# Three TensorE products with no reader, placed in the stage that transposes the cosine output

## The chip, the cores and the metric

The kernel runs on 1 core of one Trainium2 chip. The metric is the device time of one execution in microseconds; lower is better. TensorE (PE in the rows, its weight loads PEld), VectorE (DVE), ScalarE (ACT), GpSimd (POOL) and SyncE (SP) each follow a queue of their own and meet at semaphores.

## The reference

Two transformer layers on x of 32 batches x 256 rows x 128 channels, all in float32. In layer 0 two attentions and a mixture of experts read the same normalised rows:

```python
xn = layernorm(x)
Q, K = l2norm(heads(Wq)), l2norm(heads(Wk)); V = heads(Wv)        # 16 heads of 8
cos = clip(Q K^T, -0.999, 0.999)
W = maximum(1 - arccos(cos) / pi, EPS) ** 16; W = W / (sum(W) + EPS)
cosine_out = (W V) @ Wo.T + bo
softmax_out = softmax(q k^T / sqrt(8)) v
moe_out = top-2 of 8 experts of xn, weighted by the gate
x1 = x + cosine_out + softmax_out + moe_out
```

Layer 1 is a causal attention with one head of 128 and a gated feed-forward layer (352 wide) whose operands are quantised to FP4 in blocks of 16; both read layernorm(x1) and are added to x1.

## The kernel before, in words

The kernel walks the 32 batches one by one. All weights stay in SBUF: among them the identity `ident` (128x128, float32) and the experts' weights `we` (128 x 8 x 128). The work on a batch is cut into stages, and the table `ORDER` writes out by hand, for each engine, in which order the stages stand in one turn of the loop and for which batch: an entry (stage, part, lag) of turn t works on batch t + lag. Each engine follows its list strictly, so what stands behind a waiting stage waits too.

Around the change TensorE's list reads: projection 1 of the next batch, `e 1`, `finc`, `o1`, `ocT`, `e 2`, `e 3`, `wo`. The stages are:

- `e` (lines 1089 to 1098) makes softmax scores for two heads in one of two slots of `psS`. ScalarE's stage `e` (line 670) takes their exponential into `prob`; its list reads `proj 1`, `e 1`, `ln 2`, `gexp`, `e 2`, `e 3`, `guess`, `ln1`.
- `finc` (lines 1105 to 1115) transposes the sums of the cosine attention into a bank of PSUM. VectorE then adds, inverts and multiplies (lines 903, 905 and 907); the last of the three, line 907, writes the finished cosine output `oc` and brings the semaphore `s_finc` to 3 for this batch.
- `o1` (lines 1167 to 1175) is the value product of layer 1's attention for the batch before; VectorE reads it at lines 962 and 966.
- `ocT` (lines 1116 to 1123) transposes `oc`. VectorE copies the result to `ocT` (line 993).
- `wo` (lines 1124 to 1131) multiplies with Wo; VectorE adds the result to the residual as `x1` (line 921), from which layer 1 starts. All of layer 1's normalisation follows from `x1`.

VectorE's list reads `proj 1`, `gmax`, `quanth 8`, `finc`, `o1`, `ocT`, `norm`, `wo`, `ln1`. At line 797 it adds the bias to a projection that TensorE makes at line 1037.

The stages other than the scores share two banks of PSUM (`psM`), 512 float32 columns each. Uses are numbered through TensorE's list (`MISC`), and even numbers take one bank, odd ones the other. In one turn, the last use of projection 1 has number 12, `finc` 13, `o1` 14, `ocT` 15 and `wo` 16. Before a stage writes its bank it waits until the last user of that bank has been read; `bank_read` walks back two numbers and returns the semaphore and value of that reader:

```python
("down", 0, 0): (s_y, 1), ("finc", 0, 0): (s_finc, 3), ("finf", 0, 0): (s_finf, 2),
...
return psM[n % 2], n % 2
```

`due(s, b)` is the value that semaphore s has once batch b is done; `s_finc` counts 3 in a batch. `ocT` uses 256 columns of its bank (T = 256); columns 256 to 511 are not used by it.

In the rows, a float32 product shows as two matmuls, each with a weight load, and a transpose as one. Line 1145 (`p1`) is the one product in the loop whose stationary operand is 128x128 and whose moving operand has 256 columns in float32; line 1150 is the next in TensorE's queue behind it. Activations all stand at line 578, and their tiles tell them apart.

Of the kernel before, what the change touches and what calls it, by code (L numbers as in the profile page):

```python
# [111 lines left out]
def build(nc, x, Wq, Wk, Wv, Wo, bo, W_qkv, b_qkv, W_gate, b_gate, W_experts, b_experts,  # L112
          w_qkv1, w_out1, w_gate1, w_up1, w_down1, y):
    B, T, _ = x.shape
# [7 lines left out]
    with ExitStack() as ctx:  # L122
        def sb(name, shape, dt=F32):
            return ctx.enter_context(nc.sbuf_tensor(name, shape, dt))
# [11 lines left out]
        def due(s, b, n=None):  # L136

            value = b * per[s.name] + (per[s.name] if n is None else n)
            return max(value, 0) if isinstance(value, int) else value
# [15 lines left out]
        ident = sb("ident", [P, P])  # L155
# [9 lines left out]
        we = sb("we", [P, E, D])  # L165
# [164 lines left out]
        def head_window(v, k, j, head):  # L330

            e = head % 2
            return v[:, k, j, head // 2, :, :].rearrange("p t c -> p (t c)")[:, e * HALF_GROUP:e * HALF_GROUP + FULL_GROUP]

        def head_at(g, hh):

            return 8 * (g // 2) + 2 * hh + g % 2
# [17 lines left out]
        def misc_bank(stage, arg, use):  # L355
            n = MISC.index((stage, arg, use))
            return psM[n % 2], n % 2
# [17 lines left out]
        def bank_read(stage, arg, use, t, uses=MISC):  # L375

            n = uses.index((stage, arg, use))
            ring = [k for k in range(len(uses)) if k % 2 == n % 2]
            at = ring.index(n)
            for back in range(1, 4 * len(ring)):  # L380
                k, turns = ring[(at - back) % len(ring)], -((at - back) // len(ring))
                entry = t - turns + LAG[uses[k][:2]]
                if not isinstance(entry, int) or 0 <= entry < B:
                    s, event = READ[uses[k]]
                    return s, due(s, entry, event)
                if t - turns < -1:
                    break
            return s_wcp, SETUP_USES
# [610 lines left out]
        def _(pe):  # L999
            mm, transpose = nc.tensor.matmul, nc.tensor.transpose  # L1000
            pe.wait_ge(s_const, due(s_const, 0))
            pe.wait_ge(s_w, due(s_w, 0, 16 * WEIGHT_DMAS))
            for n in range(SETUP_USES):
                src, dst = (TRANSPOSES + BIAS_ROWS + PRODUCTS)[n][0], (TRANSPOSES + BIAS_ROWS + PRODUCTS)[n][-1]
                bank = psM[n % 2][0:dst.shape[0], 0:dst.shape[1]]
# [13 lines left out]
            def rows(hh):  # L1019
                return slice(FULL_GROUP * hh, FULL_GROUP * (hh + 1))  # L1020

            def run(stage, arg, b, p, t):
                if stage == "xnT":
                    bank, k = misc_bank(stage, 0, 0)
# [6 lines left out]
                if stage == "proj":  # L1031
                    pe.wait_ge(s_xnT, due(s_xnT, b))
                    for use, w, n in ((0, w0T[:, :, :].rearrange("p k n -> p (k n)"), 3 * D), (1, wf[:, :], 3 * D + E)):
                        bank, k = misc_bank(stage, arg, use)
# [3 lines left out]
                if stage == "experts":  # L1038

                    for j in range(NT):  # L1040
                        bank, k = misc_bank(stage, arg, j)
# [5 lines left out]
                if stage == "stackT":  # L1047
                    kind = KINDS[arg]
                    bank, k = misc_bank(stage, arg, 0)
# [12 lines left out]
                if stage == "c":  # L1062

                    pe.wait_ge(s_stkT, due(s_stkT, b))
                    for kt in range(NT):
                        for a in range(2):
                            hh = 2 * (arg % 2) + a
                            ins = mm(psS[:, slot, a, kt, :], stkT[rows(hh), 1, g, kt * P:(kt + 1) * P], stkT[rows(hh), 0, g, :],  # L1068
                                     start=True, stop=True)
                    ins.then_inc(s_c, 1)  # L1070
                if stage == "m":

                    pe.wait_ge(s_stkT, due(s_stkT, b, 2))
                    for qt_ in range(NT):
                        for a in range(2):
                            hh = 2 * (arg % 2) + a
                            ins = mm(psS[:, slot, a, qt_, :], stkT[rows(hh), 2, g, qt_ * P:(qt_ + 1) * P], stkT[rows(hh), 3, g, :],  # L1077
                                     start=True, stop=True)
                    ins.then_inc(s_m, 1)
                if stage == "maxT":  # L1080
                    bank, k = misc_bank(stage, 0, 0)
# [7 lines left out]
                if stage == "e":  # L1089

                    pe.wait_ge(s_mT, due(s_mT, b))
                    for kt in range(NT):
                        for a in range(2):
                            hh = 2 * (arg % 2) + a
                            mm(psS[:, slot, a, kt, :], stkT[rows(hh), 3, g, kt * P:(kt + 1) * P], stkT[rows(hh), 2, g, :],  # L1095
                               start=True, stop=False)
                            ins = mm(psS[:, slot, a, kt, :], pickb[rows(hh), g, :], mT[rows(hh), :], start=False, stop=True)  # L1097
                    ins.then_inc(s_e, 1)
                if stage == "pvf":
                    pv(arg, prob[:, 2 * (arg % 2):2 * (arg % 2) + 2, :].rearrange("p u c -> p (u c)"), vf, s_prob, 2 * arg + 2, s_pvf,  # L1100
                       b, p)
                if stage == "pvw":
                    pe.wait_ge(s_qkc, due(s_qkc, b))
                    pv(arg, curve[:, p, 2 * arg * UC:2 * (arg + 1) * UC], vc, s_pow, arg + 1, s_pvc, b, p)
                if stage in ("finc", "finf"):
                    src, ready, done = (oCs, s_oC, s_fincp) if stage == "finc" else (oFs, s_oF, s_finfp)
                    pe.wait_ge(ready, due(ready, b))
                    bank, k = misc_bank(stage, arg, 0)
# [7 lines left out]
                if stage == "ocT":  # L1116
                    bank, k = misc_bank(stage, 0, 0)
                    last, value = bank_read(stage, 0, 0, t)
                    pe.wait_ge(last, value)
                    pe.wait_ge(s_finc, due(s_finc, b))  # L1120
                    for j in range(NT):
                        ins = transpose(bank[:, j * P:(j + 1) * P], oc[:, j, :], ident[:, :])
                    ins.then_inc(s_ocTp, 1)
                if stage == "wo":
                    bank, k = misc_bank(stage, 0, 0)
# [6 lines left out]
                if stage == "xn1T":  # L1132
                    bank, k = misc_bank(stage, 0, 0)
# [6 lines left out]
                if stage == "p1":  # L1140
                    bank, k = misc_bank(stage, 0, 0)
# [4 lines left out]
                    bank, k = misc_bank(stage, 0, 1)  # L1146
# [5 lines left out]
                if stage == "s1":  # L1152
                    bank, k = misc_bank(stage, 0, 0)
# [5 lines left out]
                if stage == "p1T":  # L1159
                    bank, k = misc_bank(stage, 0, 0)  # L1160
# [6 lines left out]
                if stage == "o1":  # L1167
                    bank, k = misc_bank(stage, 0, 0)
# [7 lines left out]
                if stage == "xqT":  # L1176
                    bank, k = misc_bank(stage, 0, 0)
# [6 lines left out]
                if stage == "gu":  # L1184
                    pe.wait_ge(s_xqT, due(s_xqT, b))
                    for m in range(2):
                        bank, k = misc_bank(stage, arg, m)
# [4 lines left out]
                if stage == "hT":  # L1192
                    pe.wait_ge(s_qh, due(s_qh, b))
                    bank, k = misc_bank(stage, arg, 0)
# [5 lines left out]
                if stage == "down":  # L1200
                    bank, k = misc_bank(stage, 0, 0)
# [3 lines left out]
                    for j in range(NT):  # L1205
                        for c in range(NCH):
                            ins = mm(bank[:, j * D:(j + 1) * D], hqT[0:CH[c], j, c, :], wdT[0:CH[c], c, :],  # L1207
                                     start=(c == 0), stop=(c == NCH - 1))
                    ins.then_inc(s_dnp, 1)

            def pv(g, weights, v, ready, event, done, b, p):

                half = g // 2
                kind, copied = (0, s_oC) if v is vc else (1, s_oF)
                pe.wait_ge(ready, due(ready, b, event))
                if g == 0:
                    pe.wait_ge(copied, due(copied, b - 1))
                w = weights.rearrange("p (h k q) -> p h k q", h=4, k=NT)
                for kt in range(NT):
                    for hh in range(4):  # L1220
                        ins = mm(psV[rows(hh), kind, half, :], head_window(v, p, kt, head_at(g, hh)), w[:, hh, kt, :],  # L1221
                                 start=(g % 2 == 0 and kt == 0), stop=(g % 2 == 1 and kt == NT - 1),
                                 tile_position=(0, FULL_GROUP * hh))
                ins.then_inc(done, 1)

            steps(pe, ORDER["tensor"], run)


# [19 lines left out]
```

## Time and profile before

| what | value |
|---|---|
| median of 3 runs | 1970.91 us (1962.58 to 1976.08) |
| the profiled execution's own time | 1969.34 us |
| its span, first to last instruction | 1967.5 us |
| mean granted clock of TensorE | 0.85 of full speed |
| VectorE busy | 1766.3 us (90%) |
| ScalarE busy | 1765.2 us (90%) |
| TensorE busy (matmuls) | 1486.0 us (76%) |

A busy share is an average over the whole span. Which engine holds the others up at one place is read from the waits, the chain that ended last and the timeline there. A granted clock of 1.00 is 2.4 GHz and one of 0.50 is 1.2 GHz; values between are mixtures of the two in one stretch.

### The profile page before, as it was taken

The numbers are of one execution on the slowest core, as the hardware profiler recorded it, in microseconds if no ns is written. First come the engines' busy times: TensorE is split into PE (matmuls) and PEld (weight loads), VectorE is DVE, ScalarE is ACT, GpSimd is POOL, SyncE is SP. The second block draws the span as 40 slices with busy tenths as digits, with TensorE's granted clock in tenths as the row PEclk, the third lists the DMA queues.
The fourth block names the chain that finished last, engine by engine and source line by source line (L and its number), as shares of the span: only waits on it lengthen the run. The fifth ranks groups of instructions, "written<-read, shape, count | busy, mean of one in ns | idle before, by whom it ended". The sixth has DMA issues, their size and how long they took to land.

```text
span 1967.5 us, 38505 instructions
## 1 busy us (share of the span) xinstructions
PE 1486.0 (76%) x12022; PEld 752.9 (38%) x12022; DVE 1766.3 (90%) x4009; ACT 1765.2 (90%) x1856; POOL 1182.2 (60%) x540
## 2 busy tenths in 40 slices
PE   2667787777777877777787787878777787777766
PEld 1223434333443433344343344343334434333433
DVE  5779999999999999999999999999999999999864
ACT  1299999999999999999999999899999999999893
POOL 1566666666666566566656666665667666665640
PEclk9578889889889888888978888897888889888776
DMA  1000000000000000000000000000000000000000
GB/s 42 3 4 1 6 1 6 5 6 6 6 3 3 6 5 6 6 6 0 6 6 5 6 5 6 0 6 6 5 6 5 6 0 6 6 5 6 4 3 6
DMA packets 21058, 11.19 MB, mean 6 GB/s; under 512 B 1431, under 2 KB 20953, under 8 KB 20956
## 3 DMA queue, kind: packets, MB, share of 16 engines
q1 hardware_dynamic: 20956, 10.20, 1.8%
q14 instruction: 83, 0.68, 0.1%
q8 instruction: 19, 0.31, 0.1%
HBM read 6.00 MB, written 4.19 MB: 5 GB/s over the span
## 4 chain that ended last, share of the span: by engine, by line
DVE 34%; ACT 24%; issue 22%; PE 16%; DVEq 1%; POOL 1%; SPq 0%; ACTq 0%; DMA 0%; POOLq 0%
ACT curve L578 13%; DVE nmax L880 6%; DVE curve L870 5%; ACT root L578 4%; PE psM L1037 3%; PE psM L1045 3%; DVE curve L874 3%; DVE acc L854 2%; PE psM L1190 1%; DVE stkT L866 1%; DVE xn L776 1%; ACT prob L578 1%; ACT L609 1%; PE psS L1095 1%; DVE h L454 1%
## 5 line engine op out<-in xcount | busy, mean ns | idle before, releaser
L530 POOL TENSOR_TENSOR root<-curve 128x2048 f32<-128x2048 f32 x128 | 478.7, 3740 | 453.1 <-DVE curve L874 453.1
L578 ACT ACTIVATE curve<-curve 128x2048 f32<-128x2048 f32 x384 | 718.8, 1907 | 5.5 <-POOL curve L533 2.2
L578 ACT ACTIVATE root<-root 128x2048 f32<-128x2048 f32 x256 | 484.6, 1906 | 0.0
L533 POOL TENSOR_TENSOR curve<-curve,root 128x2048 f32<-128x2048 f32 x64 | 354.5, 5562 | 64.4 <-ACT root L578 64.4
L578 ACT ACTIVATE prob<-psS 128x1024 f32<-128x1024 f32 x256 | 256.7, 1029 | 66.1 <-PE psS L1097 63.9
L874 DVE TENSOR_SCALAR curve<-psS 128x1024 f32<-128x1024 f32 x256 | 308.4, 1216 | 2.7 <-PE psS L1068 2.7
L880 DVE TENSOR_REDUCE nmax<-psS 128x4 f32<-128x1024 f32 x256 | 303.0, 1215 | 1.0 <-PE psS L1077 1.0
L566 POOL TENSOR_TENSOR stk<-qk,stk 128x512 f16<-128x512 f32 x128 | 147.8, 1164 | 76.9 <-ACT stk L578 76.6
L1045 PE MATMUL psM<-we,xnT 128*128 128x512 f32 x256 | 168.8, 747 | 0.0
L870 DVE TENSOR_TENSOR curve<-curve,root 128x2048 f32<-128x2048 f32 x64 | 162.0, 2531 | 6.1 <-ACT root L578 6.1
L1221 PE MATMUL psV<-curve,vc 128*32 128x256 f32 x2048 | 140.8, 406 | 29.8 <-ACT curve L578 25.9
L1077 PE MATMUL psS<-stkT 32*128 32x256 f16 x1024 | 105.7, 300 | 71.5 <-DVE curve L874 36.8
L1190 PE MATMUL psM<-wguT,xqT 128*128 128x352 f32 x256 | 131.7, 654 | 36.4 <-ACT hqT L578 32.8
L1221 PE MATMUL psV<-prob,vf 128*32 128x256 f32 x2048 | 153.7, 423 | 0.6 <-ACT prob L578 0.6
L854 DVE SCALAR_TENSOR_TENSOR acc<-psM,comb,acc 128x128 f32<-128x128 f32 x512 | 137.7, 340 | 11.7 <-PE psM L1045 11.7
L1207 PE MATMUL psM<-wdT,hqT 128*128 128x128 f32 (+1 forms) x384 | 91.8, 428 | 61.8 <-DVE h L972 61.1
L1068 PE MATMUL psS<-stkT 32*128 32x256 f16 x1024 | 107.6, 314 | 21.1 <-DVE curve L874 10.4
L1207 PEld LDWEIGHTS psM<-wdT,hqT 128*128 128x128 f32 (+1 forms) x384 | 82.5, 323 | 76.5 <-DVE h L972 75.4
L1056 PE MATMUL psM<-ident,stk 128*128 128x128 f16 x1024 | 81.2, 224 | 34.3 <-ACT xn1T L578 26.6
L1095 PE MATMUL psS<-stkT 32*128 32x256 f16 x1024 | 102.3, 299 | 4.5 <-ACT prob L578 3.3
L1221 PEld LDWEIGHTS psV<-curve,vc 128*32 128x32 f32 x2048 | 61.1, 114 | 107.2 <-issue 80.2
L1097 PE MATMUL psS<-mT,pickb 32*128 32x256 bf16 x1024 | 101.4, 297 | 0.0
(194 smaller groups left out, 2800.2 us busy)
## 6 DMA issues: line engine op xcount, KB each, us to landing
xt<-in_L_attn_x SPq DMA_DIRECT2D x32, 128.0 KB, 2.1
out<-yo SPq DMA_DIRECT2D x32, 128.0 KB, 1.8
we<-in_L_ffn_W_experts SPq DMA_DIRECT2D x1, 512.0 KB
curve<-in_L_attn_w_qkv SPq DMA_DIRECT2D x1, 192.0 KB
curve<-in_L_ffn_w_down SPq DMA_DIRECT2D x1, 176.0 KB
curve<-in_L_ffn_w_gate SPq DMA_DIRECT2D x2, 64.0 KB
curve<-in_L_ffn_w_up SPq DMA_DIRECT2D x2, 64.0 KB
curve<-in_L_ffn_W_qkv SPq DMA_DIRECT2D x1, 128.0 KB
```

The costliest lines, as they stand in the source:

```text
L530: nc.gpsimd.tensor_tensor(root[:, two], curve[:, p, two], curve[:, p, two], ALU.mult).then_inc(s_sq, 1)
L533: nc.gpsimd.tensor_tensor(curve[:, p, two], curve[:, p, two], root[:, two], ALU.mult).then_inc(s_half[0], 1)
L566: nc.gpsimd.tensor_tensor(lo, src, hi, ALU.subtract).then_inc(s_stk, 1)
L578: return nc.scalar.activation(out, in_, func, **kw)
L854: nc.vector.scalar_tensor_tensor(acc[:, p, j, :], bank[:, (e % 4) * D:(e % 4 + 1) * D], comb[:, p, j, e:e + 1], acc[:, p, j, :], ALU.mult, ...
L870: nc.vector.tensor_tensor(curve[:, p, two], curve[:, p, two], root[:, two], ALU.mult).then_inc(s_half[1], 1)
L874: nc.vector.tensor_scalar(curve[:, p, arg * UC:(arg + 1) * UC], psS[:, slot_of(stage, arg), :, :, :].rearrange("p a k q -> p (a k q)"), CO ...
L880: nc.vector.tensor_reduce(nmax[:, :, 2 * arg:2 * arg + 2].rearrange("p j a -> p a j"), psS[:, slot_of(stage, arg), :, :, :], AX.X, ALU.max ...
L1045: mm(bank[:, :], xnT[:, j * P:(j + 1) * P], we[:, 4 * arg:4 * arg + 4, :].rearrange("p e f -> p (e f)"), start=False, stop=True).then_inc( ...
L1190: ins = mm(bank[:, 0:I], xqT[:, arg * P:(arg + 1) * P], wguT[:, m, :], start=True, stop=True)
L1207: ins = mm(bank[:, j * D:(j + 1) * D], hqT[0:CH[c], j, c, :], wdT[0:CH[c], c, :], start=(c == 0), stop=(c == NCH - 1))
L1221: ins = mm(psV[rows(hh), kind, half, :], head_window(v, p, kt, head_at(g, hh)), w[:, hh, kt, :], start=(g % 2 == 0 and kt == 0), stop=(g % ...
```

## The change

In the stage `ocT`, between the wait for the bank and the wait for the cosine output, TensorE runs three products of `ident` with the first two experts' weights (256 columns). They are written to columns 256 to 511 of the stage's bank, each over the one before, and nothing reads them.

```diff
                     bank, k = misc_bank(stage, 0, 0)
                     last, value = bank_read(stage, 0, 0, t)
                     pe.wait_ge(last, value)
+                    keep_clock(bank[:, T:2 * T], 3)
                     pe.wait_ge(s_finc, due(s_finc, b))
                     for j in range(NT):
                         ins = transpose(bank[:, j * P:(j + 1) * P], oc[:, j, :], ident[:, :])
                     ins.then_inc(s_ocTp, 1)
...
+            def keep_clock(spare_psum, count):
+
+                for k in range(count):
+                    mm(spare_psum, ident[:, :], we[:, 0:2, :].rearrange("p e f -> p (e f)"), start=True, stop=True)
```

## Rows read from the trace of the kernel before

**Rows 1.** The page: busy time of each engine, share of the span, instructions.

```profile
PE 1486.0 (76%) x12022; PEld 752.9 (38%) x12022; DVE 1766.3 (90%) x4009; ACT 1765.2 (90%) x1856; POOL 1182.2 (60%) x540
```

**Rows 2.** Waits, whole span: who waited for whom, us in total, times, longest.

```profile
ACT prob L578 <- PE psS L1097: 63.9, 77, 1.8
...
DVE qk L797 <- PE psM L1037: 61.0, 40, 4.3
...
PE psM L1122 <- DVE oc L907: 51.3, 30, 2.1
```

**Rows 3.** Chain that ended last, 1070 to 1082 us: start, us, what.

```profile
1075.46 0.44 DVE oc L907
...
1076.03 0.41 PE psM L1122 x2
1076.44 0.24 PE psS L1095 x4
```

**Rows 4.** Timeline, 323 to 328 us: start, length, instruction, [idle before <-releaser].

```profile
323.53 0.39 PE L1175 MATMUL psM<-v,p1T 128*128 128x129 f32 x2
...
324.97 0.42 DVE L907 TENSOR_TENSOR oc<-psM,rsC 128x256 f32<-128x256 f32 x1
...
325.55 0.41 PE L1122 MATMUL psM<-ident,oc 128*128 128x128 f32 x2 [1.63 <-DVE oc L907]
...
326.04 0.42 DVE L993 COPY ocT<-psM 128x256 f32<-128x256 f32 x1
...
326.55 1.94 ACT L578 ACTIVATE prob<-psS 128x1024 f32<-128x1024 f32 x2 [0.92 <-PE psS L1097]
...
327.41 0.42 DVE L921 TENSOR_TENSOR x<-psM,acc 128x256 f32<-128x256 f32 x1
```

**Rows 5.** Timeline, 381 to 386 us: the same stage one batch later.

```profile
381.97 0.42 DVE L907 TENSOR_TENSOR oc<-psM,rsC 128x256 f32<-128x256 f32 x1
...
382.54 0.66 PE L1122 MATMUL psM<-ident,oc 128*128 128x128 f32 x2 [1.88 <-DVE oc L907]
...
384.21 1.94 ACT L578 ACTIVATE prob<-psS 128x1024 f32<-128x1024 f32 x2 [1.84 <-PE psS L1097]
...
385.43 0.41 DVE L921 TENSOR_TENSOR x<-psM,acc 128x256 f32<-128x256 f32 x1
```

**Rows 6.** Stretches between ends of line 907: length; PE, PEld, DVE, ACT, POOL busy; clock.

```profile
325.39:382.39 57.00, 44.22 (x375) 22.62 (x375) 53.59 (x125) 54.86 (x59) 36.98 (x17) 0.88 0.02 5
382.39:440.46 58.07, 45.61 (x375) 23.30 (x375) 54.85 (x125) 54.83 (x57) 36.76 (x17) 0.85 0.02 5
728.01:785.08 57.07, 44.27 (x375) 22.62 (x375) 53.73 (x125) 55.15 (x59) 36.86 (x17) 0.88 0.02 5
785.08:843.11 58.03, 45.60 (x375) 23.24 (x375) 54.64 (x124) 54.91 (x58) 36.77 (x17) 0.85 0.02 5
```

**Rows 7.** The same columns, for 0.9 and for 2.0 us from line 907's end.

```profile
382.39:383.29 0.90, 0.75 (x6) 0.45 (x10) 0.74 (x5) 0.00 (x0) 0.90 (x1) 0.51 0.00 0
...
1933.50:1934.40 0.90, 0.81 (x3) 0.29 (x2) 0.69 (x4) 0.00 (x0) 0.00 (x0) 0.50 0.00 0
...
152.35:154.35 2.00, 1.81 (x22) 1.32 (x22) 1.37 (x4) 1.70 (x3) 2.00 (x3) 0.84 0.00 0
...
1933.50:1935.50 2.00, 1.33 (x5) 0.84 (x5) 1.12 (x5) 0.00 (x0) 0.00 (x0) 0.50 0.00 0
```

**Rows 8.** Line 1145 in all (ns min/median/max), and two timelines.

```profile
L1145 PE MATMUL psM<-xn1T,wqk x64: 379/468/763, 164.1 to 1941.2; 128*128 128x256 f32 x64
...
1086.63 0.70 PE L1145 MATMUL psM<-xn1T,wqk 128*128 128x256 f32 x2
1087.17 0.61 PE L1150 MATMUL psM<-wvo,xn1T 128*128 128x128 f32 x4
...
1940.61 1.19 PE L1145 MATMUL psM<-xn1T,wqk 128*128 128x256 f32 x2 [0.56 <-ACT xn1T L578]
...
1941.59 1.06 PE L1150 MATMUL psM<-wvo,xn1T 128*128 128x128 f32 x4
```

## The prediction, made before the change was run

> **What bounds the kernel now.** I read the page first. VectorE and ScalarE are both busy for 90% of the span, TensorE for 76% [rows 1]. Shares don't say who waits at the place of the change, so the view of the waits came next. It has both sides of the stage `ocT` near its top: TensorE waits 51.3 us in all for the cosine output (line 907), and ScalarE waits 63.9 us for scores (line 1097) [rows 2]. The chain that ended last shows that these are one story: from line 907 it goes to the two transposes at line 1122, and on to the scores at line 1095 that stand behind them in TensorE's queue [rows 3].
>
> The timeline of one batch has the times [rows 4]. The last product of `o1` ends at 323.92 us (323.53 + 0.39), line 907 ends at 325.39, and the transposes start at 325.55: TensorE idled 1.63 us. The exponential of `e 2` starts at 326.55, and ScalarE had stood idle for 0.92 us, because `e 2` is queued behind the transposes. VectorE's copy at line 993 starts at 326.04 with no idle time ahead of it, and `x1` (line 921) follows at 327.41. So VectorE has next to no slack here, and ScalarE has less than none.
>
> Is a delay at this place passed on to the next batch? The trace holds a test. One batch later the granted clock is 0.51 in the stretch right behind line 907 [rows 7], so the same work is late [rows 5]: line 907 ends at 382.39, and the exponential starts 1.82 us behind it instead of 1.16, `x1` 3.04 us behind it instead of 2.02. The first batch lasted 57.00 us from line 907 to line 907, the one that was slowed 58.07; another such pair has 57.07 and 58.03 [rows 6]. A delay of 0.7 us for ScalarE and 1.0 us for `x1` made the batch 1.0 us longer. Nothing later took it back: ScalarE's idle time outside this one wait is 57.00 - 54.86 - 0.92 = 1.22 us in the first batch and 58.07 - 54.83 - 1.84 = 1.40 us in the second [rows 4 to 6].
>
> **What the change does.** It means to fill TensorE's 1.63 us of idling. What decides is when the wait ahead of the products ends. It waits for the reader of the bank's last user. The uses alternate between two banks, and `finc` has number 13, `o1` 14, `ocT` 15. So the last user of `ocT`'s bank is `finc` of the same batch, and its reader is done when `s_finc` stands at 3, which is the end of line 907. The wait behind the products asks for the same value of the same semaphore. **Both waits end together, and the three products run after the wait and not in it.** The idling stays whole, and the products stand between the cosine output and the transposes.
>
> A rule of the Trainium skill says why no earlier wait would do ("PSUM — Partial Sum Buffer", section "PSUM bank collisions raise a hardware error"): engines have to be kept apart by bank and quadrant, not by address, so the unused columns of a bank that VectorE is reading are not free to write. No row of before shows what happens otherwise.
>
> **The price of the products.** Each batch gets three products, which are six matmuls and six weight loads. The nearest row has the same shape, line 1145. At full clock its two matmuls take 0.54 us until line 1150 starts (1086.63 to 1087.17). The second one ends at 1087.33 and lasts 0.38, so it started 0.32 us behind the first, and line 1150 came 0.22 us after that [rows 8]. In a run of six, I take it that only the first has the longer step, since the later weight loads lie under the matmul ahead: 0.32 + 5 x 0.22 = 1.42 us. The other end is 3 x 0.54 = 1.62 us, every pair like that at line 1145. I take 1.42. At the low clock the pair takes 0.98 us (1940.61 to 1941.59) [rows 8], so three cost at most 2.94, and by twice 1.42 they cost 2.84.
>
> Nothing is removed or moved, and there is no DMA, no new wait and no new semaphore. `ident` and `we` lie in SBUF. The second wait is met already when TensorE comes to it; I cost it at nothing, since TensorE's queue is then full of the products.
>
> **Who pays.** The transposes, `e 2`, `e 3` and `wo` start 1.42 us later. ScalarE's wait for `e 2` grows from 0.92 to about 2.3 us in the batch shown, and VectorE waits about 1.4 us at line 993 where it waited for nothing. Both are late together. VectorE has another wait in the batch, at line 797, of 1.5 us on average (61.0 / 40) [rows 2]. That one is for a projection whose operand ScalarE copies, and ScalarE is just as late, so it doesn't take the delay back. With a delay passed on in full, 32 x 1.42 = **45 us**.
>
> **The clock.** In the 0.9 us behind line 907 the granted clock is below 1.00 in 11 of the 32 batches, and in the 2.0 us behind it in 20; the first and the last of each are shown [rows 7]. Two things follow, with opposite signs.
> - Against: in the 11 batches the products cost 2.84 us and not 1.42, at most 11 x 1.42 = 16 us. Most of that is not new: while the products use up the time at the low clock, the transposes and scores behind them get less of it, and it cost them 1.0 us in such a batch before [rows 6]. In the other 9 the fall now meets the transposes and scores, at up to 1.0 us each, 9 us. I take 20 us for the sum at its worst.
> - For: the products are work where there was none so early, and could keep the clock from falling. At 1.0 us for each of the 20 batches [rows 6, 7] that is 20 us at most. It can't reach a fall that comes at the end of line 907 itself [rows 5, 7], because no product has run by then.
>
> I take zero for the sum of the two, and keep -20 and +20 for the range. The forecast is 1969.3 + 45 = **2014 us** against the profiled execution's 1969.34, which lies 1.6 us below the median of the runs.
>
> **Rivals.**
> 1. *The clock is held.* For it: the clock falls behind an idle stretch, at a place where the products add work. The cost remains, 45 - 20 = +25 us, **1994 us**. The skill has a rule on this side ("TensorE: Matmul & The Clock Gate", section "What's actually happening"): the low level is the default, and activity lifts it. That the clock is low behind this wait in 20 batches [rows 7] agrees with it; by it alone the time would be this rival's.
> 2. *The delay is absorbed: not slower.* VectorE's 1.5 us at line 797 [rows 2] and ScalarE's other 1.2 to 1.4 us of idling in a batch [rows 4 to 6] are of the size of the delay. They would hide it if each engine took its own share back there. It decides if less than 0.44 of the delay is passed on (19.7 of 45 us). The time would lie between 1969 and 1989 us, **1979 us** in the middle. Against it stand the two pairs of batches, which passed on all of it [rows 6].
> 3. *The clock gets worse.* If the low level comes at the end of line 907 in every batch, the products cost 32 x 2.84 = 91 us, less 1.0 us for each of the 20 batches that paid for it before: +71 us, **2040 us**.
> 4. *It does what it says.* If the first wait ended earlier, the products would lie in the 1.63 us of idling and cost next to nothing, and up to 20 us of low clock would go: **1955 us**, with 14 us in place of 20. The numbering of the banks speaks against it.
>
> **How the numbers follow.** Forecast 0.68, rival 1 0.13, rival 2 0.11, rival 3 0.05, rival 4 0.03. 1% of the median is 19.7 us, about what a measurement of this kernel can tell from no change, so the border is at 1990.6 us. The forecast, rival 3 and most of rival 1 lie above it: slower 0.86. Rival 2 lies within 1%: 0.11. Faster by over 1% is rival 4: 0.03. The range goes from 1988 us (rival 1 with 6 us of the delay absorbed) to 2036 us (the forecast with the full +20 of the clock).
>
> **What would show it.** In the profile after, the matmuls of the new line start about 0.15 us behind the end of line 907, not behind the last product of `o1`, and the idling ahead of them is still put down to line 907. From line 907's end to the transposes it is some 1.6 us and not 0.16. ScalarE's wait for line 1097 grows by about 45 us in all, VectorE waits at line 993, and a batch lasts about 59 us. I am wrong if the products start while line 907 still runs, if a batch lasts no longer although the transposes are late (absorbed), or if the granted clock behind line 907 changes in so many batches that it outweighs 45 us.

## The result, and the profile after

The change made the kernel slower: 2002.77 us in the median of four executions (1995.63 to 2019.77) against 1971.35 us before. The ratio is 1.0177, with an interval of 1.01 to 1.0254. The forecast was 2014 us, its range 1988 to 2036. The direction and the size were right. The composition was not: in the profiled execution most of the time was lost in four of the 32 batches, by something that the prediction didn't know of, while the delay that it counted cost on balance a quarter of what it said. When the same kernel was measured again (experiment 9) its ratio was 1.0075; there two of five executions, 2013.87 and 2050.23 us, lie over 1.5% above the fastest and are left out as disturbed, though no trace says whether they were that or had more of those long batches.

The profiled execution after is the slowest of the four, 2019.77 us, 50.43 us above the one before (1969.34). All readings of after are from it. Its page, as [rows 1], with the span:

```profile
span 2018.0 us, 38857 instructions
...
PE 1521.1 (75%) x12214; PEld 783.0 (39%) x12214; DVE 1760.7 (87%) x4009; ACT 1761.7 (87%) x1856; POOL 1181.4 (59%) x540
```

VectorE and ScalarE are busy 5.6 and 3.5 us less than in [rows 1], in an execution that is 50 us longer. The 192 new matmuls are TensorE's. The loss shows as idle time of VectorE and ScalarE, and the waits say where, as in [rows 2]:

```profile
ACT prob L578 <- PE psS L1097: 86.5, 64, 4.0
...
DVE qk L797 <- PE psM L1037: 56.6, 35, 4.3
```

ScalarE's wait for scores grew by 22.6 us (from 63.9), where 45 was expected. VectorE's wait at line 797 fell from 61.0 to 56.6, and at line 993, where it had waited 1.6 us in all, it waits 43.6. The timeline of one batch, the counterpart of [rows 4] (start, length, instruction, idle before and its releaser; line 1215 is the products, line 1123 the transposes, line 1176 the last of `o1`):

```profile
1367.65 0.39 PE L1176 MATMUL psM<-v,p1T 128*128 128x129 f32 x2
...
1369.06 0.42 DVE L907 TENSOR_TENSOR oc<-psM,rsC 128x256 f32<-128x256 f32 x1
...
1369.54 1.56 PE L1215 MATMUL psM<-we,ident 128*128 128x256 f32 x6 [1.50 <-DVE oc L907]
...
1370.94 0.38 PE L1123 MATMUL psM<-ident,oc 128*128 128x128 f32 x2
...
1371.36 0.42 DVE L993 COPY ocT<-psM 128x256 f32<-128x256 f32 x1 [1.15 <-PE psM L1123]
...
1371.91 1.94 ACT L578 ACTIVATE prob<-psS 128x1024 f32<-128x1024 f32 x2 [2.15 <-PE psS L1097]
```

The products do not run in the wait. They start at 1369.54, 0.06 us behind line 907's end (1369.06 + 0.42 = 1369.48), and the 1.50 us of idling ahead of them is still put down to line 907. The transposes come 1.46 us behind line 907 instead of 0.16 [rows 4], so they are 1.30 us late. The exponential of `e 2` starts 2.43 us behind line 907 instead of 1.16, so 1.27 us late.

The stretches from one end of line 907 to the next, as in [rows 6]:

```profile
1311.33:1369.47 58.14, 45.84 (x381) 23.95 (x381) 53.64 (x125) 54.35 (x57) 36.80 (x17) 0.88 0.02 5
1369.47:1427.29 57.82, 45.81 (x381) 23.85 (x381) 53.00 (x125) 54.33 (x58) 36.80 (x17) 0.88 0.02 5
1427.29:1494.13 66.84, 52.99 (x381) 25.51 (x381) 57.96 (x125) 55.29 (x59) 36.57 (x17) 0.74 0.01 4
1494.13:1553.57 59.44, 47.47 (x381) 24.78 (x381) 52.99 (x125) 54.12 (x57) 36.77 (x17) 0.86 0.02 5
```

Here is the surprise. A quiet batch lasts 58 us; before, the 27 batches in the middle lasted 57.72 on average. Four batches last 66.7 to 66.9 us, at 1427, 1553, 1680 and 1806, and the one behind each of the first three about 59.45. Over the 31 stretches the sum rose from 1781.15 to 1830.53 us, by 49.4. Four times about 8.8 us over a quiet batch of 58.0 and three times 1.5 us make 40 us of it. The quiet batches together lost only some 10 us.

What makes a batch long? In the third row VectorE is busy for 4 to 5 us more with the same 125 instructions, so one of them took longer. The timeline of a quiet batch has the pair that matters:

```profile
1384.37 0.16 DVE L839 TENSOR_TENSOR ge<-ge,left 128x16 f32<-128x16 f32 x1
...
1385.00 4.54 POOL L533 TENSOR_TENSOR curve<-curve,root 128x2048 f32<-128x2048 f32 x1 [1.66 <-ACT root L578]
```

And the same place in the long batch:

```profile
1439.91 2.36 DVE L880 TENSOR_REDUCE nmax<-psS 128x4 f32<-128x1024 f32 x2 [0.58 <-PE psS L1077]
...
1442.82 4.51 POOL L533 TENSOR_TENSOR curve<-curve,root 128x2048 f32<-128x2048 f32 x1 [1.66 <-ACT root L578]
1442.85 4.50 DVE L839 TENSOR_TENSOR ge<-ge,left 128x16 f32<-128x16 f32 x1
```

Line 839 works on 16 elements a partition, in the top-2 choice of the gate, and takes 0.16 us. In the quiet batch it starts 0.63 us ahead of GpSimd's big multiplication at line 533. In the long one VectorE had waited 0.58 us at line 880 for scores, line 839 started 0.03 us behind line 533, and it ended with it, 4.50 us later. Everything behind it on VectorE stood still. Before, the longest of line 839's 32 executions took 0.346 us (shortest, median and longest in ns):

```profile
L839 DVE TENSOR_TENSOR ge<-ge,left x32: 159/163/346, 60.8 to 1842.5; 128x16 f32<-128x16 f32 x32
```

The hold itself is 4.3 of the 8.8 us. In the rest of such a batch the granted clock is lower as well (0.74 in the third row, 0.88 in those ahead of it); how the other 4.5 us divide was not told apart.

### The profile page after: what moved, and what is told of

It is laid out like the page before. It is cut to its first block, busy times and chain, and to the rows that moved or that the text cites. A ratio compares the mean times of both kernels' runs of the same rounds, so it can differ in the third digit from the quotient of the medians.

```text
span 2018.0 us, 38857 instructions
## 1 busy us (share of the span) xinstructions
PE 1521.1 (75%) x12214; PEld 783.0 (39%) x12214; DVE 1760.7 (87%) x4009; ACT 1761.7 (87%) x1856; POOL 1181.4 (59%) x540
## 4 chain that ended last, share of the span: by engine, by line
ACT 33%; DVE 23%; issue 21%; PE 19%; DVEq 1%; POOL 1%; ACTq 1%; SPq 0%; DMA 0%; POOLq 0%
ACT curve L578 19%; ACT root L578 6%; DVE nmax L880 4%; PE psM L1037 3%; PE psM L1215 3%; PE psM L1045 2%; DVE curve L870 2%; PE psM L1191 2%; PE psV L1227 2%; ACT prob L578 2%; ACT L609 2%; DVE curve L874 1%; DVE stkT L866 1%; DVE xn L776 1%; PE psS L1095 1%
## 5 line engine op out<-in xcount | busy, mean ns | idle before, releaser
L880 DVE TENSOR_REDUCE nmax<-psS 128x4 f32<-128x1024 f32 x256 | 303.0, 1215 | 7.0 <-PE psS L1077 7.0
L1191 PE MATMUL psM<-wguT,xqT 128*128 128x352 f32 x256 | 142.0, 697 | 34.4 <-ACT hqT L578 29.1
L1227 PE MATMUL psV<-prob,vf 128*32 128x256 f32 x2048 | 147.8, 409 | 0.6 <-ACT prob L578 0.6
L1208 PE MATMUL psM<-wdT,hqT 128*128 128x128 f32 (+1 forms) x384 | 86.3, 409 | 60.1 <-DVE h L972 59.4
L1056 PE MATMUL psM<-ident,stk 128*128 128x128 f16 x1024 | 85.9, 232 | 33.2 <-ACT xn1T L578 26.3
L1208 PEld LDWEIGHTS psM<-wdT,hqT 128*128 128x128 f32 (+1 forms) x384 | 77.4, 305 | 73.8 <-DVE h L972 72.7
L549 POOL TENSOR_TENSOR qk<-qk,rn 128x512 f32<-128x512 f32 x32 | 34.5, 1078 | 113.6 <-DVE rn L821 113.6
```

The source lines that it names most:

```text
L880: nc.vector.tensor_reduce(nmax[:, :, 2 * arg:2 * arg + 2].rearrange("p j a -> p a j"), psS[:, slot_of(stage, arg), :, :, :], AX.X, ALU.max ...
L1191: ins = mm(bank[:, 0:I], xqT[:, arg * P:(arg + 1) * P], wguT[:, m, :], start=True, stop=True)
```

## The experiments

Each ratio is the time against the kernel before in the same set of runs, with its 95% interval.

**1. The products in the wait itself.** They go ahead of the wait for the bank and write into the free slot of `psS` that `e 2` uses next.

```diff
+                    last, value = bank_read("e", 2, 0, t, SCORES)
+                    pe.wait_ge(last, value)
+                    keep_clock(psS[:, slot_of("e", 2), 0, 0, :], 3)
                     bank, k = misc_bank(stage, 0, 0)
                     last, value = bank_read(stage, 0, 0, t)
                     pe.wait_ge(last, value)
-                    keep_clock(bank[:, T:2 * T], 3)
```

> The same three products, but issued ahead of the wait for the cosine output, into a bank of the scores that is free by then, so that they run while TensorE idles. Theory A (the cost of the change is the delay of the transposes by 1.3 us): the delay is gone, the transposes start 0.16 us behind line 907 as before, and the ratio is 0.99 to 1.00. Theory B (the products themselves cost, wherever they stand): ratio 1.01 to 1.02. If the clock is held as well, it is 1.00 in the 2 us behind line 907 in nearly all batches, against 12 of 32 before.

Measured: 1.0005 [0.9976, 1.0035], 1976.53 us against 1973.06.

```profile
954.79 1.73 DVE L454 TENSOR_TENSOR h<-h,qa 128x704 f32<-128x704 f32 x1
...
955.15 0.39 PE L1178 MATMUL psM<-v,p1T 128*128 128x129 f32 x2
...
955.37 1.46 PE L1217 MATMUL psS<-we,ident 128*128 128x256 f32 x6
...
957.05 0.42 DVE L907 TENSOR_TENSOR oc<-psM,rsC 128x256 f32<-128x256 f32 x1
...
957.62 0.41 PE L1125 MATMUL psM<-ident,oc 128*128 128x128 f32 x2 [0.79 <-DVE oc L907]
```

The products (line 1217) follow `o1` with no gap, the transposes come 0.15 us behind line 907 as before, and the idling is half as long. So it is the place of the wait that made the delay. But the kernel gained nothing, though the granted clock behind line 907 is below 1.00 in 2 batches only, where it was in 20 before. The batches show why:

```profile
898.40:957.51 59.11, 46.54 (x381) 24.25 (x381) 53.79 (x124) 54.95 (x58) 38.90 (x19) 0.86 0.02 5
957.51:1014.45 56.94, 45.69 (x381) 23.27 (x381) 53.88 (x124) 54.71 (x57) 34.78 (x15) 0.88 0.02 5
```

From 725 us on nearly every second batch lasts 59.1 us, and the others 57.0. In 12 batches line 454 takes 1.73 us, as in the timeline above, and 0.88 in the others. Each time it had started 0.05 to 0.07 us behind a start of GpSimd's line 557. Lines 903 to 907 follow it in VectorE's queue, and so the cosine output is late.

**2. Another kind of work, same place.** Ten transposes in place of the three products, in the same bank.

```diff
-                    keep_clock(bank[:, T:2 * T], 3)
+                    keep_clock(bank[:, T:2 * T], 10)
...
-                    mm(spare_psum, ident[:, :], we[:, 0:2, :].rearrange("p e f -> p (e f)"), start=True, stop=True)
+                    transpose(spare_psum[:, 0:P], we[:, 0, :], ident[:, :])
```

> Ten transposes of 128 columns take the place of the three products, at the same place behind the wait: about the same delay (1.2 us) without a product. Theory A (delay alone): ratio 1.01 to 1.02, like the change. Theory C (the products held the clock behind line 907, and that gave back part of the delay): the clock falls again in 10 to 20 batches behind line 907, ordinary batches last 58.3 to 58.8 us instead of 58.0, ratio 1.02 to 1.035.

Measured: 1.0137 [1.0073, 1.0201], 1999.26 us. Four batches of 63.3 to 63.4 us; the clock is below 1.00 behind line 907 in 9 batches. Line 839, all 32 executions:

```profile
L839 DVE TENSOR_TENSOR ge<-ge,left x32: 159/164/4510, 60.6 to 1876.7; 128x16 f32<-128x16 f32 x32
```

A like loss with other filler, which makes the transposes 1.05 us late: the long batches don't need the products.

**3. The change, with line 839 out of the way.** The step `choose 3`, which contains line 839, goes a few places earlier in VectorE's order, so that it is done well before line 533 starts.

```diff
-        ("quantx", 5, -1), ("quantx", 6, -1), ("stackT", 1, 1), ("choose", 2, 1), ("quantx", 7, -1), ("m", 0, 1),
-        ("m", 1, 1), ("quantx", 8, -1), ("p1", 0, -1), ("choose", 3, 1), ("m", 2, 1), ("stackT", 2, 1),
+        ("quantx", 5, -1), ("quantx", 6, -1), ("stackT", 1, 1), ("choose", 2, 1), ("quantx", 7, -1), ("choose", 3, 1), ("m", 0, 1),
+        ("m", 1, 1), ("quantx", 8, -1), ("p1", 0, -1), ("m", 2, 1), ("stackT", 2, 1),
```

Between `quantx 7` and `m 0` is its new place.

> The change, with one short VectorE instruction (line 839, 16 elements) moved a few places earlier in VectorE's list. Theory D (most of the profiled cost is four batches of 66.8 us, in which line 839 comes behind the start of a GpSimd multiplication and is held for 4.5 us): no batch is over 60 us but those of the ends, batches last about 58.0 us, and the ratio is 1.005 to 1.01. Theory A (delay alone): the long batches are by the way, and the ratio stays at 1.015 to 1.02.

Measured: 1.0041 [1.0026, 1.0055], 1980.46 us, and the five executions lie within 1979.1 to 1983.57, where those of the change lie within 24 us. Line 839 takes 0.71 us at most, and there is no long batch:

```profile
963.65:1021.76 58.11, 45.84 (x381) 23.98 (x381) 53.62 (x124) 54.32 (x56) 36.77 (x17) 0.88 0.02 5
1021.76:1079.59 57.83, 45.85 (x381) 23.89 (x381) 53.03 (x124) 54.34 (x58) 36.80 (x17) 0.88 0.02 5
```

So line 839's hold, with what follows from it, is the difference between 1.0177 and 1.0041 (between 1.0075 and 1.0041 in the repeat). What is left is the cost of the delay on balance, 10.3 us in the sum of the 31 stretches (1791.48 against 1781.15), for 31 x 1.28 = 40 us of delay.

**4. Twice the dose.** Six products.

```diff
-                    keep_clock(bank[:, T:2 * T], 3)
+                    keep_clock(bank[:, T:2 * T], 6)
```

> Six products instead of three, at the same place: the transposes start 2.7 us behind line 907. Theory A with the delay passed on in full: twice the cost, 32 x 2.7 = 86 us, ratio 1.044. Theory E (about 1 us of a delay is absorbed by other waits of ScalarE, what goes beyond is passed on): batches of 59.0 to 59.5 us, 1.4 us over those of three products, ratio 1.025 to 1.035 without long batches.

Measured: 1.0334 [1.0317, 1.0351], 2038.83 us, with line 839 never over 0.31 us. The quiet batches last 59.1 to 59.3 us, others up to 63.2. A product takes 0.43 us there, so the second three add 1.3 us, and they cost 1.2 us in a quiet batch, nearly all of it. The first three cost 0.3 (58.0 against 57.72), but against an average batch that has delays of its own; the section on the prediction compares like with like.

**5. The control for 3.** The kernel before, with `choose 3` moved alone.

> The kernel before, with line 839 moved earlier as in the third experiment: its control. Theory D (the move only takes away a collision that the kernel before doesn't have): ratio 0.998 to 1.002. If the move is a gain by itself, then 0.99, and the third experiment would have hidden a cost of the change of that size.

Measured: 1.0015 [1.0, 1.003], 1975.76 us against 1972.73. The move by itself costs 0.0 to 0.3%, so experiment 3 is not fast because the move is a gain of its own. The clock is below 1.00 behind line 907 in 21 batches, as before.

**6. A third of the dose.** One product, and `choose 3` moved as in experiment 3.

```diff
-                    keep_clock(bank[:, T:2 * T], 3)
+                    keep_clock(bank[:, T:2 * T], 1)
```

> One product instead of three, with line 839 moved as in the third experiment, so that its collision can't come in. The transposes start 0.15 + 0.5 us behind line 907. Theory F (a delay is passed on nearly in full, counted from a batch of 56.9 us that meets no fall of the clock behind line 907 and no collision, and the change gives most of it back because it takes away such falls): quiet batches of 57.3 to 57.5 us; ratio 0.995 to 1.00 if the falls stay away, 1.00 to 1.005 if they come back. Theory E (the first microsecond of a delay is absorbed): quiet batches of 56.9 us.

Measured: 1.003 [1.0018, 1.0041], 1978.02 us. One product costs almost what three do. Behind the first, its batches run from 57.4 to 59.3 us up to the last two, so none is as short as the 56.9 us that were expected if the first microsecond of a delay were absorbed. Line 809, which makes 6.7 us in all in experiment 3, makes 29.1 here, and `x1` stands behind it: the transposes are only 0.44 us late, but `x1` mostly starts 3.04 us behind line 907, where it was 2.02 in [rows 4]. So a shorter delay is not a smaller loss in proportion. The clock is below 1.00 in 6 batches.

**7. Useful work in the wait.** No products; `e 2` goes ahead of `ocT` in TensorE's order.

```diff
-("o1", 0, -2), ("ocT", 0, -1), ("e", 2, 0), ("e", 3, 0), ("wo", 0, -1),
+("o1", 0, -2), ("e", 2, 0), ("ocT", 0, -1), ("e", 3, 0), ("wo", 0, -1),
```

> The kernel before, with the scores of stage e 2 ahead of the stage that waits for the cosine output, so that useful work fills the idling. If ScalarE's wait for e 2 is what a batch pays for here: it goes from 1.1 us to near zero, and the ratio is 0.98 to 0.99. If VectorE's chain behind the cosine output sets the end, nothing moves: ratio 0.995 to 1.005.

Measured: 1.0346 [1.0293, 1.0398], 2038.0 us. ScalarE's wait for scores was halved, but another, for `xqT` (4.4 us before), took its place:

```profile
ACT xqT L578 <- PE psM L1182: 79.5, 22, 5.4
...
ACT prob L578 <- PE psS L1097: 30.5, 63, 1.5
```

Line 839 was held again, 14 times for 4.45 to 4.51 us, and 14 batches last 62 to 65 us.

**8. An earlier cosine output.** VectorE's `quanth 8` (line 454) moves from ahead of `finc` to behind `ln1`, in the kernel before.

```diff
-        ("quanth", 7, -2), ("c", 7, 0), ("proj", 0, 1), ("proj", 1, 1), ("gmax", 0, 1), ("quanth", 8, -2),
-        ("finc", 0, -1), ("o1", 0, -2), ("ocT", 0, -1), ("norm", 0, 1), ("wo", 0, -1), ("ln1", 0, -1),
+        ("quanth", 7, -2), ("c", 7, 0), ("proj", 0, 1), ("proj", 1, 1), ("gmax", 0, 1),
+        ("finc", 0, -1), ("o1", 0, -2), ("ocT", 0, -1), ("norm", 0, 1), ("wo", 0, -1), ("ln1", 0, -1), ("quanth", 8, -2),
```

> The kernel before, with VectorE's last quantisation step (line 454 of stage quanth 8, 0.88 us) moved from ahead of the cosine output's three instructions to behind the statistics of ln1. The cosine output is finished 0.88 us earlier, and TensorE's idling ahead of the transposes shrinks from 1.5 to 0.6 us. If a delay at this place is passed on, so is this gain: 0.6 to 0.9 us per batch, ratio 0.985 to 0.99. If other waits take it: 0.995 to 1.00.

Measured: 1.001 [0.9996, 1.0025], 1974.49 us. The clock is below 1.00 behind line 907 in 3 batches only, and again nothing is gained: line 454, at its new place, makes 54.2 us in all instead of 30.7.

**9. The change again.** The same kernel, for the spread.

> The change itself once more. Theory D (its time is the sum of quiet batches of 58.0 us and of a number of long ones that differs from run to run): ratio 1.01 to 1.025, single times apart by 10 us or more, and in the profile every batch over 60 us is one in which line 839 lasts 4.5 us. Theory A (delay alone): times within 0.5% of one another.

Measured: 1.0075 [1.0048, 1.0101], median 1987.48 us of 1981.4, 1986.71, 1987.48, 2013.87 and 2050.23. The profiled execution (1987.48) has one long batch, of 63.68 us, and one execution of line 839 of 4.49 us; its 31 stretches sum to 1798.24, 17.1 us above before. That is 10 us for the delay and 7 for one long batch and its successor. With all five executions the mean is 2003.9 us.

**10 and 11. The useful work again, with line 839 cleared.** Number 10 is experiment 7 with `choose 3` behind both of GpSimd's multiplications. Number 11 adds the move of experiment 8.

```diff
-("o1", 0, -2), ("ocT", 0, -1), ("e", 2, 0), ("e", 3, 0), ("wo", 0, -1),
+("o1", 0, -2), ("e", 2, 0), ("ocT", 0, -1), ("e", 3, 0), ("wo", 0, -1),
...
-("p1", 0, -1), ("choose", 3, 1), ("m", 2, 1), ("stackT", 2, 1),
+("p1", 0, -1), ("m", 2, 1), ("stackT", 2, 1),
...
-("hmul", 1, -1), ("choose", 4, 1), ("quanth", 0, -1), ("c", 1, 1)
+("hmul", 1, -1), ("choose", 3, 1), ("quanth", 0, -1), ("choose", 4, 1), ("c", 1, 1)
```

> The scores of stage e 2 ahead of the cosine output's transposes, as in the seventh experiment, with line 839 moved behind both of GpSimd's multiplications. Theory D: no batch is long because of line 839, quiet batches last 56.4 to 57.5 us as they did there, and the ratio is 0.98 to 0.995. If something else made the seventh experiment slow, it stays above 1.01.

> The same with line 454 behind the statistics of ln1 as in the eighth experiment: both waits of the cosine output shortened. If they add up: quiet batches of 56 us, ratio 0.97 to 0.985. If another stage sets the end by then: the same as with e 2 alone.

Measured: 1.003 [1.0011, 1.0049] and 0.9993 [0.9975, 1.0011]. Line 839 takes 0.17 us at most in both, so experiment 7's loss was mainly its hold. Yet ScalarE's shorter wait for scores is no gain, since it waits elsewhere. In number 10:

```profile
ACT xqT L578 <- PE psM L1182: 31.1, 25, 2.3
ACT prob L578 <- PE psS L1097: 26.0, 61, 1.7
...
ACT u1T L578 <- PE psM L1145: 15.8, 21, 1.4
```

Before, it waited 4.4 us for `xqT`. VectorE makes the operand of `xqT`, and one step of that, line 450, was held in its turn. In 20 batches it took 1.41 to 1.43 us, each time 0.01 to 0.03 us behind a start of GpSimd's line 566; before, it took 0.43 at most and 13.6 in all.

```profile
L450 DVE SCALAR_TENSOR_TENSOR xq<-xqT,xq 128x256 f32<-128x256 f32 x32 | 33.5, 1046 | 1.1
```

In number 11 line 450 is at 13.6 us again and line 454, at its new place, makes 53.5.

No version beats the kernel before by more than the measurement can tell.

**12. VectorE late alone.** No products; VectorE does a reduction that nothing reads (1.21 us) just ahead of its wait for `ocT`. It was to tell whether a VectorE that is late is simply held less by GpSimd.

```diff
+        pad = sb("pad", [P, 1])
...
+                    nc.vector.tensor_reduce(pad[:, :], we[:, :, :], AX.XY, ALU.max)
```

> The kernel before, with no product, in which VectorE alone is made late: a reduction of 1024 elements that nothing reads (about 1.1 us) ahead of its copy at line 993. TensorE's transposes and the scores of e 2 are not late. Theory G (a late VectorE is held less by GpSimd: line 452 of quantx 7 falls from 25 us in all to 15, line 809 from 14 to 7, as in the change, and this takes back part of the delay): ratio 1.00 to 1.007, line 452 near 15 us. Theory A (every delay on this path is passed on in full): 32 x 1.1 = 35 us, ratio 1.018, line 452 near 25 us. Line 839 can come under GpSimd's multiplication here as well; batches in which it lasts 4.5 us are counted apart.

Measured: 1.0488 [1.045, 1.0526], 2068.8 us against 1974.64: 94 us for 38.7 us of added work. Lines 453, 455 and 558 here are 452, 454 and 557 of the others:

```profile
L455 DVE TENSOR_TENSOR h<-h,qa 128x704 f32<-128x704 f32 x32 | 47.8, 1492 | 0.1
...
L992 DVE TENSOR_REDUCE pad<-we 128x1 f32<-128x1024 f32 x32 | 38.7, 1209 | 0.0
L453 DVE SCALAR_TENSOR_TENSOR xq<-xqT,xq 128x256 f32<-128x256 f32 x32 | 38.2, 1194 | 0.1
```

That theory fell. VectorE was held more and not less: lines 453 and 455 make 86.0 us, against 56.0 before. Of the two lines that it named only 809 fell as it had said, from 14.0 to 8.1 us. In 23 batches on end line 455 takes 1.73 us, each time 0.06 to 0.07 us behind a start of GpSimd's line 558, and those batches last 61.4 to 61.5 us. A delay that falls badly against GpSimd comes back batch after batch there. The two sizes add up to 69 of the 94 us if all of them lie on the path; the rest is open.

## Why the prediction was right, and where it was wrong

**Both waits end together: right.** The products start 0.06 us behind line 907, not 0.15 us behind as said, and never in the wait. Rival 4 is out. Experiment 1 shows the reverse, the same products in the wait and no delay. Whether the other half of the bank could have been written while VectorE reads the first was not tried, so for the Trainium skill's rule ("PSUM — Partial Sum Buffer", section "PSUM bank collisions raise a hardware error") that engines are kept apart by bank and quadrant and not by address, no run here shows what happens otherwise.

**The price: right, slightly high.** 1.42 us was predicted, 1.28 measured as delay of the transposes and of `e 2`.

**45 us of delay on top of the time before: wrong, and this is the step that failed.** The term was 32 x 1.42 = 45 us, with the delay passed on in full. Without the collision at line 839 the kernel lost 10.3 us (experiment 3), a quarter of the 40 us of delay. Two things can be behind this: the test of the passing-on was misread, or the term was added to the wrong time.

The test holds. In its slowed batch [rows 5, 6] another thing was late as well, which the rows shown there leave out:

```profile
384.29 1.22 DVE L809 TENSOR_SCALAR n<-n 128x64 f32<-128x64 f32 x1
384.31 2.27 POOL L566 TENSOR_TENSOR stk<-qk,stk 128x512 f16<-128x512 f32 x2
```

The median of line 809 is 0.32 us. In four batches of before, both slowed ones of [rows 6] among them, it met GpSimd's line 566 and took 1.22, and `x1` (line 921) stands behind it in VectorE's queue. But four other batches were slowed by the low clock without that hold. One of them, in the columns of [rows 7], [rows 4] and [rows 6]:

```profile
843.11:845.11 2.00, 1.85 (x19) 1.08 (x20) 1.81 (x7) 0.18 (x1) 2.00 (x3) 0.52 0.00 0
...
845.01 0.20 DVE L809 TENSOR_SCALAR n<-n 128x64 f32<-128x64 f32 x1
846.10 0.42 DVE L921 TENSOR_TENSOR x<-psM,acc 128x256 f32<-128x256 f32 x1 [0.90 <-PE psM L1130]
...
843.11:901.21 58.10, 45.81 (x375) 23.36 (x375) 53.97 (x125) 54.81 (x57) 36.80 (x17) 0.85 0.02 5
```

Line 809 takes 0.20 us, VectorE waits 0.90 us for TensorE instead, `x1` starts 2.99 us behind line 907 and the batch lasts as long, 58.10 us.

The time was the wrong one. The 57.72 us of an average batch have delays of other kinds in them, and the change did away with these. The 27 batches in the middle of before, each counted once, by what was late in it:

| batches of before | how many | mean length |
|---|---|---|
| clock 1.00 in the 2.0 us behind line 907, and none of lines 452, 454, 809 and 839 held | 7 | 56.95 us (56.54 to 57.57) |
| clock 0.50 to 0.54 there, with or without a hold | 8 | 58.1 us |
| line 454 held, 1.73 to 1.76 us | 3 | 58.8 us |
| line 452 held, 1.16 to 1.30 us (clock 0.86 to 1.00) | 9 | 57.6 us |

In experiment 3 all 27 are of the first kind, and they last 58.00 us in the mean. So like against like the delay of 1.28 us costs 1.05 us a batch, 28 us in the 27. The other 20 batches of before had cost 21 us, and their delays are gone; that leaves some 8 us in the 27 and 10.3 in all 31. By experiment 5, where line 839 stands at its new place as well, the delay costs 0.85 us (five batches of the first kind, 57.15 us). Experiment 4 has 20 of the first kind, which last 59.3 us, 2.35 more than 56.95 for 2.6 us of delay. In these single traces, then, some 0.65 to 0.9 of the delay is passed on. What fails is to add it to a mean over batches that are late for other reasons.

VectorE's groups show the same from its side, before (first fence) and in experiment 3 (second; total us, mean ns, idle before):

```profile
L454 DVE TENSOR_TENSOR h<-h,qa 128x704 f32<-128x704 f32 x32 | 30.7, 960 | 0.1
...
L452 DVE SCALAR_TENSOR_TENSOR xq<-xqT,xq 128x256 f32<-128x256 f32 x32 | 25.3, 791 | 0.1
L809 DVE TENSOR_SCALAR n<-n 128x64 f32<-128x64 f32 x32 | 14.0, 438 | 1.1
...
L993 DVE COPY ocT<-psM 128x256 f32<-128x256 f32 x32 | 13.4, 418 | 1.6 <-PE psM L1122 0.6
```

```profile
L454 DVE TENSOR_TENSOR h<-h,qa 128x704 f32<-128x704 f32 x32 | 28.1, 879 | 0.1
L452 DVE SCALAR_TENSOR_TENSOR xq<-xqT,xq 128x256 f32<-128x256 f32 x32 | 15.5, 484 | 0.1
...
L993 DVE COPY ocT<-psM 128x256 f32<-128x256 f32 x32 | 13.6, 425 | 39.4 <-PE psM L1123 39.4
...
L809 DVE TENSOR_SCALAR n<-n 128x64 f32<-128x64 f32 x32 | 6.7, 210 | 1.1
```

VectorE waits 37.8 us more at line 993. It is busy 21.7 us less (1766.3 before, 1744.6 in experiment 3), of which lines 454, 452 and 809 make 2.6, 9.8 and 7.3. Its other waits shrink by 4.9 us. That leaves 11.2 us, which is what the span grew by (1967.5 to 1978.7).

Line 452 works on 256 columns in 0.45 us when GpSimd doesn't hold it; before, it took up to 1.30, each long execution ending 0.28 us behind an instruction of GpSimd's line 566 that had started just ahead of it. In experiment 3 its longest is 0.54. What moved these lines clear of GpSimd was not told apart. Line 452 falls to 15.0 us also in experiment 8, which has neither product nor delay, and not in experiment 10 (20.8 us), where the clock is below 1.00 in 6 batches only. Line 809 stays at 13.1 us in experiment 2, whose delay is nearly that of the change.

**The clock, taken as zero: wrong, and rival 1 had the mechanism.** Behind line 907 the granted clock is below 1.00 in 5 of 32 batches after, 3 in the repeat and 2 in experiment 3, against 20 in [rows 7]. One of the 5, in the columns of [rows 7]:

```profile
1494.13:1496.13 2.00, 1.93 (x5) 1.59 (x6) 0.70 (x4) 0.08 (x1) 2.00 (x3) 0.58 0.00 0
```

The mean clock of the whole execution went from 0.850 to 0.886 in experiment 3. The products did keep the clock up there, as rival 1 said. That agrees with the rule of the Trainium skill that activity lifts the clock ("TensorE: Matmul & The Clock Gate", section "What's actually happening"); the time that it gave by itself, 1994 us, is not what was measured without line 839's hold. The prediction also held that a fall at the end of line 907 itself was out of reach, as no product has run by then. Yet in the 0.9 us behind line 907 too the clock is below 1.00 in 2 batches of experiment 3, against 11 before; why is open. But a held clock is not by itself time: experiments 1 and 8 had it held (2 and 3 batches) without the delay, and gained nothing, since GpSimd held VectorE's line 454 longer instead. Of rival 2, 1979 us, the size came true without line 839's hold (1980.46 us), but not the mechanism: all of VectorE's waits other than line 993 took back 4.9 us. The upper end of the range was added up wrongly as well: 2014 + 20 is 2034 us and not 2036.

**The hold of line 839: not foreseen.** It brought the time back up to where the forecast was, and so made the forecast right for a wrong reason, by luck: the repeat, with one such hold in its trace, has its median at 1987.48 us, just below the range. The mechanism is the one on which the Trainium skill has a rule ("SBUF — State Buffer", section "Who interferes with whom"): VectorE and GpSimd share a pair of SBUF ports as an exclusive lock, a VectorE instruction with two SBUF inputs contends with a GpSimd one that reads SBUF, and the one that comes first blocks the other for its whole length. The trace agrees: line 839 reads `ge` and `left` from SBUF, and when it started 0.03 us behind line 533 it ended with it, after 4.50 us. When it started 0.63 us ahead, it took 0.16. The delay alone doesn't use up that margin in each batch, as 28 of 32 batches show; in the long batch shown, a wait for TensorE at line 880 did. Why just these batches have that wait, one in the repeat and four in the first profile, is open, and so is what set the times of the executions without a trace.

## What to carry to other kernels

Work that is meant to fill a wait has to be free of that wait: before it is placed, look up which semaphore value its own output buffer waits for. A delay in a tightly packed kernel isn't a number that is added to the mean turn; it moves short instructions of one engine against long ones of another, so list the margins between the two and see which of them the delay uses up. And a pass-on rate that is read from two turns counts from an undisturbed turn: sort the turns by what is late in them first, and ask which of those delays the new one replaces.

## What the runs showed of the hardware

A VectorE instruction on 128x16 elements took 0.16 us free and 4.50 us when it started 0.03 us behind a GpSimd multiplication of 128x2048; 14 such holds in one execution went with a kernel slower by 3.5% (experiment 7). A one-operand instruction was held as well: line 809 on 128x64 took 1.22 us when it started within 0.02 us of GpSimd's line 566, and 0.20 to 0.32 in most batches. The granted clock fell to 0.50 (1.2 GHz) behind a wait in which TensorE idled 1.88 us [rows 5, 7]. Filling that wait with products or shortening it (experiments 1 and 8) left 2 and 3 of these falls, of 20, without making the kernel faster.
